# Three loops over the turns written out in full, on all engines, in a four-layer graph network

## What is computed

```python
x = _layernorm(x + _L0_gnn_ref(x, adj, adj, ...))   # graph mixing, 4-head attention, an MLP of 512
x = _layernorm(x + _L1_gnn_ref(x, adj, ...))        # two graph mixings, then LSTMs over windows of 1 to 4 nodes
x = _layernorm(x + _L2_gnn_ref(x, adj, ...))        # graph mixing, two products with batch norms over all rows
x = _layernorm(x + _L3_gnn_ref(x, adj, adj, ...))   # attention with masks, mixing with the parents' matrix
```

## Time and profile before

| | us |
|---|---|
| median of 3 runs | 2211.63 |
| lowest and highest run | 2209.86, 2214.37 |
| profiled execution, its own time | 2209.12 |
| its span, first to last instruction | 2207.3 |
| around the span (2209.12 - 2207.3) | 1.8 |
| PE busy within the span | 2110.7 (96%) |

### The profile page before, as it was taken

One profiled execution on the slowest core, in us unless ns is written; L12 is line 12 of the kernel. 1 busy time (PEld: TensorE's weight loads), 2 busy tenths in 40 slices (PEclk: granted clock), 3 DMA queues, 4 the chain that ended last, 5 costly groups with the idle time before them and its releaser, 6 DMA issues. The chain is left out here.

```text
span 2207.3 us, 45637 instructions
## 1 busy us (share of the span) xinstructions
PE 2110.7 (96%) x17941; PEld 1845.5 (84%) x17941; DVE 1371.8 (62%) x2737; ACT 1159.1 (53%) x2184; POOL 474.7 (22%) x1131
## 2 busy tenths in 40 slices
PE   6999999999969989999999999999999899899998
PEld 5898888889859978888888999988888799777886
DVE  5788888888866645443344344344344488876775
ACT  1454464455434357644445344353443477657887
POOL 3555565565540000000000000000000132003343
PEclk9999999999989999999999999999999999998999
DMA  4001101111132101000000000000000143001333
GB/s 127 16 30 41 59 30 40 49 55 35 40 103 65 57 31 39 1 20 1 1 1 20 20 1 1 1 1 20 0 1 1 38 130 114 6 20 42 83 86 77
DMA packets 77041, 82.65 MB, mean 37 GB/s; under 512 B 7136, under 2 KB 74592, under 8 KB 76000
## 3 DMA queue, kind: packets, MB, share of 16 engines
q1 hardware_dynamic: 76896, 80.53, 12.1%
HBM read 55.34 MB, written 25.17 MB: 36 GB/s over the span
## 5 line engine op out<-in xcount | busy, mean ns | idle before, releaser
L336 PE MATMUL ps<-R 128*128 128x256 f32 (+3 forms) x8136 | 1491.3, 343 | 13.8 <-DVE R L1465 7.4
L336 PEld LDWEIGHTS ps<-R 128*128 128x128 f32 x8136 | 1309.5, 190 | 172.0 <-issue 9.2
L1411 ACT ACTIVATE late_half<-ps,lstm_bias 128x512 f32<-128x512 f32 (+2 forms) x460 | 283.0, 669 | 376.2 <-PE ps L336 376.1
L378 POOL TENSOR_TENSOR ln_veps<-ln_mv,eps_tile 128x2 f32<-128x2 f32 x128 | 24.9, 195 | 1180.3 <-DVE ln_mv L361 1180.3
L305 POOL TENSOR_TENSOR H<-H 128x128 f32<-128x128 f32 x384 | 203.9, 563 | 1.4 <-DMA residual<-H 1.4
L1481 DVE TENSOR_TENSOR late_half<-late_half 128x1024 f32<-128x1024 f32 (+2 forms) x32 | 37.6, 1176 | 183.5 <-ACT late_half L1411 183.5
L893 PE MATMUL ps<-H 128*128 128x256 f32 x512 | 125.4, 389 | 10.2 <-issue 9.5
L1405 ACT ACTIVATE late_half<-late_half 128x1024 f32<-128x1024 f32 (+2 forms) x66 | 68.1, 1032 | 124.6 <-DVE late_half L1486 78.5
L917 PE MATMUL ps<-H 128*128 128x256 f32 x512 | 120.3, 380 | 0.0
L1483 DVE TENSOR_TENSOR late_half<-late_half 128x1024 f32<-128x1024 f32 (+2 forms) x32 | 37.6, 1176 | 131.3 <-ACT late_half L1411 131.3
L893 PEld LDWEIGHTS ps<-H 128*128 128x128 f32 x512 | 94.3, 194 | 22.8 <-issue 10.6
(11 more groups left out here) (213 smaller groups left out, 2536.8 us busy)
## 6 DMA issues: line engine op xcount, KB each, us to landing
H<-in_x SPq DMA_DIRECT2D x64, 256.0 KB, 2.9
residual<-H SPq DMA_DIRECT2D x32, 256.0 KB, 2.2
H<-residual SPq DMA_DIRECT2D x32, 256.0 KB, 3.9
arena<-residual SPq DMA_DIRECT2D x32, 256.0 KB, 2.7
residual<-arena SPq DMA_DIRECT2D x32, 256.0 KB, 2.2
H_state<-residual SPq DMA_DIRECT2D x32, 256.0 KB, 2.8
out<-H_state SPq DMA_DIRECT2D x64, 128.0 KB, 2.4
arena<-in_wih SPq DMA_DIRECT2D x4, 1024.0 KB, 4.8
```

The lines of the kernel that those rows point to most:

```text
L336: mm = pe.matmul(out, lhsT(a), rhs(b), start=start and n == 0, stop=stop and n == len(PASSES) - 1)
L1411: ins = act.activation(into[q][:, m, 0:x.cols], gate_ps(q, m, x.cols), ACT.Tanh if q == TANH_G else ACT.Sigmoid, bias=lstm_bias[:, x.p - 1 ...
```

## The change

In `weave` the hardware loop is gone; the rounds between are written out like the first and the last. All three calls of `weave` on each engine are touched, so blocks 1, 3 and 4 change and block 2 keeps its loops. The order of the slots, the waits and the buffers stay as they are.

```diff
-    for i in range(-1, late):
-        round_of(i)
-    with eng.Fori(late, turns - 1) as i:
-        round_of(i)
-    for i in range(turns - 1, turns + late):
+    for i in range(-1, turns + late):
         round_of(i)
```

## The result

The changed kernel takes 2195.09 us (median of 4 runs, 2193.90 to 2196.28) against 2210.74 us before in the same comparison: 15.65 us less, a ratio of 0.9929 of the medians. The ratio that has a 95% interval, given for the experiments too, is 0.9923 (0.9910 to 0.9935). The direction was forecast. The size was not: I had 11.5 us and a range that ended at 2195.5, and the time lies 0.4 us outside it.

A forecast was written before the change was run, and what follows sets the result against it. PE, busy 96% of the span, was taken to bound the kernel; 11.2 (block 1) + 0 (block 3) + 0.3 (block 4) + 0 (other engines) = 11.5 us off 2211.6 gave 2200.1 us, range 2195.5 to 2206.5.

The forecast's parts named there:

- Block 1's rounds: First layer: five looped turns each lose 2.245 us against written-out ones, so 11.2 us come back.
- The half-gain rival: Block 1: DVE catches up in PE's pause, so only 5.6 us plus 0.3 come, 2205.7 us; chance 0.12.
- fourth rival: Bounds left at zero all come, 1.5 us in block 3 and 1.2 for DVE: 2197.4 us; chance 0.06.
- DVE's pauses: PE's waits for DVE in block 1, 1.9 us in all: gain taken as 0, at most 1.2 us.
- Blocks 3 and 4: Third layer's rounds and last layer: 0 gained in block 3, 0.3 us from block 4's five branches.
- The upper bound of 1.5 us: Block 3: six branches at 0.24 us each, after block 2's pauses; 0 was taken, as no pause is seen.
- the page's rule: PE holds 2048 instructions, so block 1's round would be held and its five branches worth 0.5 us.
- Theory J: Follow-up forecast: place decides; block 1's loop moved to 224 has 208 ns branches, 72.97 us rounds, 11 us less in block 1.
- The third rival: Blocks 3 and 4: 22 more instruction packets could each stall PE some 2.0 us, 44 us slower, 2244 us; chance 0.06.

The follow-up runs named there:

- The 86 increments: The changed kernel with 86 semaphore increments on PE behind its last work of block 1, moving block 2's loop from place 102 to 188; 2199.74 us, ratio 0.9949.
- the one with 256 increments: The kernel before, loops kept, with 256 semaphore increments on PE behind its last work of block 1, leaving block 2's loop at place 188; 2234.93 us.
- 110 idle instructions on PE: The kernel before, all loops kept, with 110 semaphore increments spread over PE's idle time in the prologue; 2197.73 us against 2212.68, ratio 0.9928.

## Why the prediction was wrong

**Block 1's rounds** were right: 11.4 us against 11.2, by the comparison of whole turns. That PE's branch is the cause, that the pauses need nothing from the other engines, and that DVE, ACT and POOL keep up at 73 us a round, the runs show directly. The half-gain rival has no support.

**The step that failed is a term that isn't in the sum.** Block 2 keeps its loops, and the sum has no term for it, which puts it at nothing. But the change puts 8106 more instructions ahead of block 2 on PE, and the place of a loop among the groups of 256 has a price: at 188 a group ends 8 instructions behind the branch's target, and each later turn takes 0.18 us more; in the first turn there is a pause of 1.4 to 2.2 us for a group that isn't there. Block 2 gained 3.8 us of the 15.3. Of these 1.3 are the seven later turns (114.2 us before, 112.9 after) and 1.5 the pause. The last 1.0 us isn't shown to be the place's: the granted clock rose 4.4 us behind block 2's first matmul before and 2.9 us behind it after, ahead of the pause in either case. The 86 increments that undo the place bring block 2 to 135.6 us and the kernel to 2199.7, 4.65 us above the changed one. I had a row for it: the "issue" entry for L336 is among PE's waits in the whole kernel before, and the seven of L292 that I used in the earlier trace rows were read from a window that begins behind it.

```profile
PE ps L336 <- issue: 1.5, 1, 1.5
```

That the time fell outside the range is in part chance. The kernel before took 2210.74 us in this comparison and not 2211.63, and of the 5.0 us between 2200.1 and 2195.1 this is 0.9. A gain of 15.65 us from 2211.6 would have ended at 2196.0, inside the range. The other 4.1 us are gain that the sum doesn't have. The range allowed for them without a reason: its fourth rival looks for more gain in block 3 and in DVE's pauses, and neither gave any that can be seen.

**Blocks 3 and 4.** Block 4's seven turns gained 0.37 us where I had 0.3. In block 3 a round takes 16.51 us instead of 16.52, so nothing, as said. The upper bound of 1.5 us there was empty. What I expected to see brought in is there: 2 packets a round in block 4 (2041.7:2066.9), and no pause from it.

```profile
q8 instruction: 2, 0.03, 0.6%
q14 instruction: 1, 0.01, 0.2%
```

**The mechanism was half right.** I said that the round of block 1 is too large to be held and set this against the page's rule. The runs show that size alone is not it: 1636 instructions are held when the loop begins at 224, and are brought in again each round when it begins at 114. So what I called a disagreement with the Trainium skill ("Runtime: NRT & Kernel Launch", section "Instruction fetch mechanics") was none. Its 2048 instructions for PE, in blocks of 256, are 8 blocks, and they fit the counts above: 7 groups of the body and the one behind it are 8, and the body at 114 needs 9. The page asks of a branch's target that it lie in the "current 2-page window"; I had taken that as all that PE holds, and the short branches over bodies of 717 to 1531 instructions, more than two blocks of 256, bear this reading out. By that page the store is refilled in order, so the next block pushes out the oldest; which block pushed out the loop's first one is argued from the page and not shown by a run. What is shown is 9 packets a round at one place and none at the other. The expectation of Theory J says that the loop of before ends almost at a group's end; by the counts it ends 18 instructions behind one.

**The third rival** (straight code arrives too late) I gave 0.06 for blocks 3 and 4. There it doesn't happen. In block 2, which the change leaves alone, it does when that block is written out as well, and the kernel is 6.5 us slower than the changed one. What I missed is that the rate matters within a burst: 512 instructions in 4.2 us, where block 4 runs as many in 25 us.

**A price that the profile of before didn't show.** A pause has a second price that this profile of before happens not to show. In the run with blocks 3 and 4 written out, the round behind the first branch takes 77.12 us instead of some 75. Its timeline there, and the window behind the pause:

```profile
187.94 0.60 PE L929 MATMUL ps<-ident,H 128*128 128x128 f32 x4
190.72 3.25 PE L897 MATMUL ps<-H 128*128 128x256 f32 x8 [2.19 <-issue]
```

```profile
191.30:194.70 3.40, 3.40 (x10) 2.65 (x9) 0.69 (x1) 0.00 (x0) 0.00 (x0) 0.50 0.19 64
```

After 2.2 us of standing still the granted clock is 0.50 for 3.4 us, the 1.2 GHz level, and the eight matmuls take 3.25 us instead of 1.89. Of the seven profiled kernels with the long branch five have one such round, of 76.97 to 77.45 us, the kernel before and the one with 256 increments none. Of the seven without it none has one. The pause's length alone doesn't decide it: pauses of 2.04 to 2.54 us stand ahead of the five drops, and the one of 2.38 us in the kernel with 256 increments has no drop behind it. As an estimate, 5 of 7 at 2 us each, a median of before carries some 1.4 us that its profiled execution does not. The medians differ by 15.65 us and the profiled executions by 15.2, so at most a part of it reaches the result; the cause of those 0.4 us isn't settled. Block 2's first turn varies in the same way, from 17.5 to 22.2 us, with the time at which the clock rises behind the barrier. Its pause can have the second price too. In five of the seven kernels with block 2's loop at 188 the clock falls once more behind it (0.51 at 665.7:669.2 with blocks 3 and 4 written out), but not in the kernel before nor in the changed one with 86 more; in the six with the loop at 102 or 42, which have no such pause, it never does.

## What to carry to other kernels

Before a loop is written out because its branch is long, look at whether the branch waits for instructions (packets of instructions in a looped round), and whether moving the loop's start among the groups of 256 makes it short: 110 idle instructions on PE did here what 13,562 more of them, written out, did. Compare every stage of the two traces, the untouched ones first, since a change of an engine's code moves everything behind it. Write out a loop only where its instructions are used up slowly: in these runs straight code at 45 ns an instruction (1636 in 73 us) had no pause, and bursts at 8 ns (512 in 4.2 us) did.

## What was not expected of the hardware

- The same taken branch on PE takes 0.215 us or 3.4 to 4.5 us by where the loop begins, with 1636 instructions in its body; loops of 492 to 1531 instructions never had a long one at the places tried.
- A loop with a group's end 8 instructions behind its branch's target takes PE 0.18 us more a turn (16.35 us at place 188, 16.17 at 102 and at 42), and the same place gives the same number in every kernel of the table.
- Written-out code can be slower than a loop: 16.7 to 17.6 us a turn against 16.17, with pauses of 0.8 to 1.5 us that wander by 27 or 28 matmuls from turn to turn.
- A semaphore increment on PE's queue takes some 0.16 us (110 of them move the first matmul to 17.74 us, 17.74 / 110 = 0.16).
